# Flamingo block on one core: queries and keys split by row and turned by transposing transfers

## The reference

```python
x = x + tanh(g_xattn) * xattn(layernorm(x), ctx, ctx, 16)
x = x + tanh(g_ffn) * ffn(layernorm(x), w_gate, w_up, w_down)

def xattn(q, k, v, nh):          # v isn't rotated
    q = q * cos + rotate_half(q) * sin
    k = k * cos + rotate_half(k) * sin
    scores = einsum('bqhd,bkhd->bhqk', q, k) / sqrt(32) + slope[h] * (k_pos - q_pos)
    return einsum('bhqk,bkhd->bqhd', softmax(scores), v)
```

## Time and profile before

| | us |
|---|---|
| median of 3 runs (lowest, highest) | 1881.59 (1879.17, 1883.24) |
| the profiled execution | 1877.91 |
| its span, first to last instruction | 1876.1 |

### The profile page before, as it was taken

One profiled execution on the slowest core, in us unless ns is written; L12 is line 12 of the kernel. 1 busy time (PEld: TensorE's weight loads), 2 busy tenths in 40 slices (PEclk: granted clock), 3 DMA queues, 4 the chain that ended last, 5 costly groups with the idle time before them and its releaser, 6 DMA issues. The chain is left out here.

```text
span 1876.1 us, 25013 instructions
## 1 busy us (share of the span) xinstructions
PE 1682.4 (90%) x8927; PEld 635.5 (34%) x8927; DVE 1492.9 (80%) x2119; ACT 1184.3 (63%) x1898; POOL 809.8 (43%) x442
## 2 busy tenths in 40 slices
PE   2899999999999999999986999999999930499999
PEld 0223333323333333333222444444444410244444
DVE  6899888888888888888845998968889999865551
ACT  3476777777777777776662332328896689854440
POOL 4488888978889888888540020110000000000000
PEclk9899999999999999999998999999999975799999
DMA  5576877656776667765553988848994558855552
GB/s 159 137 182 155 186 181 179 153 135 144 178 179 151 156 150 170 172 150 122 116 168 77 275 270 239 242 160 263 277 294 136 149 202 289 265 196 170 169 170 71
DMA packets 234045, 339.51 MB, mean 181 GB/s; under 512 B 74400, under 2 KB 153120, under 8 KB 225664
## 3 DMA queue, kind: packets, MB, share of 16 engines
q1 hardware_dynamic: 224992, 272.89, 48.5%
q0 software_dynamic: 8928, 65.02, 17.4%
HBM read 164.04 MB, written 92.41 MB: 137 GB/s over the span
## 5 line engine op out<-in xcount | busy, mean ns | idle before, releaser
L1111 ACT ACTIVATE P<-quad 128x512 f32<-128x512 f32 x1024 | 557.3, 599 | 229.4 <-PE quad L928 225.7
L1308 DVE TENSOR_REDUCE cm<-quad 128x1 f16<-128x1024 f32 x512 | 601.1, 1216 | 84.3 <-PE quad L916 83.0
L1837 POOL TENSOR_TENSOR Ps<-P,P 128x2048 f32<-128x2048 f32 x93 | 422.8, 4546 | 151.4 <-ACT P L1111 151.4
L928 PE MATMUL quad<-QA,KA 101*128 101x512 f16 x1024 | 352.1, 385 | 7.1 <-ACT P L1111 6.0
L916 PE MATMUL quad<-KA,QA 100*128 100x512 f16 x1024 | 327.5, 390 | 26.4 <-DVE wh L1421 6.6
L964 PE MATMUL quad<-P,cg 128*32 128x512 f32 x2048 | 272.7, 604 | 3.6 <-ACT numT L1148 0.6
L1009 PE MATMUL quad<-x_hl,Wg 128*128 128x512 f16 x1152 | 249.3, 379 | 3.0 <-DMA x_hl<-xs 3.0
L1009 PE MATMUL quad<-x_hl,Wu 128*128 128x512 f16 x1152 | 248.8, 379 | 0.0
L1054 PE MATMUL quad<-Wd,oh 128*128 128x512 f16 x768 | 228.6, 379 | 0.0
L928 PEld LDWEIGHTS quad<-QA,KA 101*128 101x128 f16 x1024 | 85.9, 97 | 298.6 <-ACT P L1111 209.6
L1195 ACT ACTIVATE ev<-quad 128x1024 f32<-128x1024 f32 x96 | 97.3, 1014 | 125.2 <-PE quad L1009 119.2
(11 more groups left out here) (158 smaller groups left out, 1926.6 us busy)
## 6 DMA issues: line engine op xcount, KB each, us to landing
Ps<-P POOLq DMA_DIRECT2D x62, 1024.0 KB, 7.8
gate_scratch<-ev SPq DMA_DIRECT2D x48, 512.0 KB, 3.8
gt<-gate_scratch SPq DMA_DIRECT2D x48, 512.0 KB, 5.5
up_scratch<-ev SPq DMA_DIRECT2D x48, 512.0 KB, 3.1
uf<-up_scratch SPq DMA_DIRECT2D x48, 512.0 KB, 5.0
uf<-up_scratch SPq DMA_DIRECT2D x96, 256.0 KB, 3.6
QA<-part_scratch SPq DMA_DIRECT2D x45, 256.0 KB
KA<-part_scratch SPq DMA_DIRECT2D x45, 256.0 KB
```

The lines of the kernel that those rows point to most:

```text
L928: e.matmul(K.score[h % 2], K.KA[p % 2][0:101, h, 128 * kt:128 * kt + 128], K.QA[p % 2][0:101, qc, h, :], start=True, stop=True).then_inc(K ...
L1111: e.activation(K.Pb[pb][:, h, :], K.score[h % 2], ACT.Exp, scale=SCALE / (QPOW * KPOW)).then_inc(K.a_exp, 1)
L1308: e.tensor_reduce(cm[:, u:u + 1], K.quad[UNIT["max", hm, u] % 2][:, :], AX.X, ALU.max).then_inc(K.v_max, 1)
L1837: e.tensor_tensor(K.Ps[n][:, :, :], K.Pb[(st.g - 1) % NP][:, :, :], K.Pb[st.g % NP][:, :, :], ALU.add).then_inc(K.g_sum, 1)
```

## The change

Queries and keys are no longer turned by TensorE. The high part (ScalarE) and the low part (VectorE) are taken row by row from the rotated values in SBUF, and written straight into a stacked tile S of four slots per head: for queries high, high, low, constant; for keys high, low, high, constant with the bias in its first four columns. A transposing transfer from S, half of the rows at a time, then writes the operand. The operands are laid out by row tile: QA and KA are [128, 8, 4, 128]. The scale 2^-6 is put into the cosine and sine tables; the factor 2 for the queries into the deviation. The bias rows are turned once by TensorE at the start.

- The rotations change places: at w = 0, 2, 6 the keys, at w = 8, 10, 14 the queries of pair p+2.
- The normalization is for pair p+2, at w = 4, 5, 6, 7 (3, 1, 3 and 1 tiles).
- The parts: keys of p+2 at w = 10 and 12, queries of p+1 at w = 0 and 2, half of the rows at each.
- The transposing transfers for pair p+1: the keys' halves at w = 0 and 1, the queries' at w = 2 and 4. Each moves 128x2048 float16.
- The load of the context columns stays at w = 1, and stands on SP's queue between the keys' two transfers.
- At the start, the row deviations of the first batch are computed in two groups of four rows, and the first queries are rotated and split in two halves.

```diff
-NORM_TILES = {10: (0, 1), 12: (2, 3, 4), 14: (5, 6), 15: (7,)}
+NORM_TILES = {4: (0, 1, 2), 5: (3,), 6: (4, 5, 6), 7: (7,)}
...
-        if w == 8 and 0 <= p and p + 2 < NQ:
-            self.turn = (p + 2, 0)
-        elif w == 0 and 0 <= p and p + 1 < NQ:
-            self.turn = (p + 1, 1)
-        elif g == -7:
-            self.turn = (1, 0)
+        self.parts = None
+        if w in (10, 12) and -1 <= p and p + 2 < NQ:
+            self.parts = (p + 2, 1, (w - 10) // 2)
+        elif w in (0, 2) and 0 <= p and p + 1 < NQ:
+            self.parts = (p + 1, 0, w // 2)
...
-            self.rope = (p + 2, k // 3, k % 3)
+            self.rope = (p + 2, 1 - k // 3, k % 3)
...
-        self.stack = (p + 1, w - 1) if 0 <= p and 1 <= w <= 2 and p + 1 < NQ else None
+        self.stack = {0: (1, 0), 1: (1, 1), 2: (0, 0), 4: (0, 1)}.get(w) if 0 <= p and p + 1 < NQ else None
...
-    def load_stack(p, w):
+    def load_stack(p, w, half):
         if p >= 2:
             e.wait_ge(K.pe_score, score_no(2 * (p - 2) + 1, 7, 3))
...
+        if w:
+            e.wait_ge(K.a_kb, p + 1)
...
+        e.wait_ge(K.a_hi, part_no(p, w, half))
+        e.wait_ge(K.v_lo, part_no(p, w, half))
+        rows = slice(4 * half, 4 * half + 4)
+        dst = (K.QA, K.KA)[w][p % 2][:, rows, :, :].rearrange("c i h t -> c (i h) t")
+        e.dma_start_transpose(dst, K.S[w][:, rows, :, :, :].rearrange("t i h n d -> t (i h n d)")).then_inc(K.d_st[w][half], 16)
...
+    def high_part(p, w, half):
+
+        if p == 0 and w == 0:
+            e.wait_ge(K.v_rope0, 4 * half + 4)
+        else:
+            e.wait_ge(K.g_rope, rope_no(p, w))
+        if p > 0:
+            e.wait_ge(K.d_st[w][half], stack_no(p - 1))
...
+            e.activation(K.S[1][:, :, :, 3, 0:4], K.biasT[:, :, :, 4 * g:4 * g + 4].rearrange("t i n h -> t i h n"), ACT.Copy).then_inc(K.a_kb, 1)
+        src = K.t1[w][:, rows, :].rearrange("t i (h d) -> t (i h) d", d=HD).unsqueeze(2).to_broadcast([128, 16, 2, HD])
+        dst = K.S[w][:, rows, :, :, :].rearrange("t i h n d -> t (i h) n d")
+        dst = dst[:, :, 0:3:2, :] if w else dst[:, :, 0:2, :]
+        e.activation(dst, src, ACT.Copy).then_inc(K.a_hi, 1)
...
     def low_part(p, w, half):
-        c = slice(512 * half, 512 * half + 512)
-        e.wait_ge(K.a_hi, turn_no(p, w, half))
...
+        e.wait_ge(K.a_hi, part_no(p, w, half))
...
+        e.scalar_tensor_tensor(dst[:, :, 2 - w, :], src, 1.0, dst[:, :, 0, :], ALU.mult, ALU.subtract).then_inc(K.v_lo, 1)
```

More of the change, by code:

```diff
@@ L619, in load_stack @@
-    def load_stack(p, w):
+    def load_stack(p, w, half):
         if p >= 2:
             e.wait_ge(K.pe_score, score_no(2 * (p - 2) + 1, 7, 3))
-        e.wait_ge(K.d_part[w], 32 * p)
-        if p == 1 and w == 0:
+        if w:
+            e.wait_ge(K.a_kb, p + 1)
+        if p == 0 and half == 0:
             e.wait_ge(K.v_aux, 2)
[L625 to L633, removed]
@@ L714, in sync_program @@
     load_x_columns(1)
[L715 to L720, removed]
+    for w, half in ((1, 0), (1, 1), (0, 0), (0, 1)):
+        load_stack(0, w, half)
     load_context(2)
@@ L746, in sync_program @@
                     e.wait_ge(K.d_wh[h][i], 16 * 6)
-            e.wait_ge(K.d_st[1], 112 * 8)
+            for i in range(2):
+                for j in range(2):
+                    e.wait_ge(K.d_st[i][j], stack_no(NQ - 1))
             for i in range(2):
@@ L938, in tensor_program @@
     e.wait_ge(K.d_id, 16)
-    for w in (1, 0):
-        turn(0, w)
-    e.wait_ge(K.a_aux, 2)
+    e.wait_ge(K.d_bias, 16)
+    for i in range(8):
+        mm = e.transpose(K.score[0][:, 32 * i:32 * i + 32], K.bias[:, 128 * i:128 * i + 128], ident[0:32, 0:32])
+    mm.then_inc(K.pe_bias, 1)
     before = None
@@ L975, in tensor_program @@
                 mm.then_inc(done, 1)
-        if st.turn is not None:
-            turn(*st.turn)
         for job in st.side:
@@ L1157, in scalar_program @@
             exponent(st.hf, st.s, 3)
-        if st.turn is not None:
-            turned(*st.turn, 0)
-            turned(*st.turn, 1)
+        if st.parts is not None:
+            high_part(*st.parts)
         for job in st.side:
@@ L1317, in low_part @@
     def low_part(p, w, half):
[L1318 to L1328 removed]
+        rows = slice(4 * half, 4 * half + 4)
+        e.wait_ge(K.a_hi, part_no(p, w, half))
+        if p > 0:
+            e.wait_ge(K.d_st[w][half], stack_no(p - 1))
+        dst = K.S[w][:, rows, :, :, :].rearrange("t i h n d -> t (i h) n d")
+        src = K.t1[w][:, rows, :].rearrange("t i (h d) -> t (i h) d", d=HD)
+        e.scalar_tensor_tensor(dst[:, :, 2 - w, :], src, 1.0, dst[:, :, 0, :], ALU.mult, ALU.subtract).then_inc(K.v_lo, 1)
     def centre_x(n):
@@ L1337, in vector_program @@
         e.memset(K.cm[i][:, :], 0.0).then_inc(K.v_cm, 1)
+    e.memset(K.S[0][:, :, :, 3, :], QPOW * KPOW).then_inc(K.v_aux, 1)
+    e.memset(K.S[1][:, :, :, 3, :], -1.0).then_inc(K.v_aux, 1)
+    e.wait_ge(K.d_cs, 32)
+    for table in (K.cos, K.sin):
+        e.tensor_scalar(table[:, :, :], table[:, :, :], KPOW, None, ALU.mult).then_inc(K.v_cs, 1)
+    e.wait_ge(K.pe_bias, 1)
+    e.wait_ge(K.a_bias, 1)
+    bias = K.score[0][:, 0:256].rearrange("t (i n h) -> t i n h", n=2, h=16)
+    e.tensor_tensor(K.biasT[:, :, 2:4, :], bias, K.biasT[:, :, 0:2, :], ALU.subtract).then_inc(K.v_bias, 1)
@@ L1744, in gpsimd_program @@
     e.memset(K.seventh[:, :], 1.0 / 7.0).then_inc(K.g_half, 1)
+    e.memset(K.twice[:, :], QPOW / KPOW).then_inc(K.g_half, 1)
     e.memset(K.ones[:, :], 1.0).then_inc(K.g_ones, 1)
-    for part in range(3):
-        rope(0, 1, part)
     def step_of(out, a, b, op, sem, count):
```

265 lines of the change are left out of this document (102 added, 163 removed).

## The result

| | before | after |
|---|---|---|
| median, us (lowest to highest, runs) | 1881.24 (1879.17 to 1883.24, 4) | 1981.6 (1975.65 to 1996.85, 4) |
| profiled execution | 1877.91 | 1980.46 |
| its span | 1876.1 | 1977.6 |

The ratio is 1.0546, 95% interval 1.0485 to 1.0606. Forecast were 1881 and a range of 1860 to 1900; the change costs 100 us. Where the runs of one kernel spread, a ratio is taken from those within 1.5% of its fastest.

A forecast was written before the change was run, and what follows sets the result against it. TensorE was taken to bound attention. Terms: -34 (turns) -1.6 (key stack) +3 (ScalarE) +8 (VectorE) +25 (context) +2 (later accumulations) -3 (start) = -0.6 us, giving 1881 us on the median; range for 8 in 10, 1860 to 1900.

The forecast's parts named there:

- A low part reads SBUF instead of PSUM: VectorE's low parts: the source was given no price, since the same kind from SBUF takes 684 ns.
- the context wait: GpSimd's keys' rotation waits some 4 us for context columns, delaying the accumulating DMA and step 6's denominators on TensorE: +25.
- Steps 0 and 8: TensorE's steps with and without a turn: each turn costs 1.24 us; removing 29 gives -34, step 0 at 2.88.
- rival (c): TensorE isn't the bound, so the turns give nothing back: +33, 1915 us; chance 0.04.
- ScalarE's high part: Writes every value twice, 1.05 us four times a pair; about 0.2 us stick out at step 0: +3.
- Step 14: VectorE's low part at step 12 pushes the following maxima, so step 14 waits 0.6 us in 14 pairs: +8.
- The wait for the key stack of pair 1: The first maxima's wait of 1.61 us goes, since pair 1's keys are turned before step 0: -1.6.
- The start: Before the steps: constant rows and TensorE's turns go, row deviations and three transfers come: -3, bounds -8 and +5.
- upper bound for this stretch, 33.4: From step 0 to the accumulating DMA's landing, both landings at their most: 33.4 us, 10 a pair, 130 in all.
- Cost nothing: Four transposing transfers of 3.0 us a pair replace DRAM stores and seven loads, at no cost.
- Rival (b): Transposing transfers hold the engines, delaying context and accumulating DMA; 1.3 us more in 13 pairs gives 1898; chance 0.26.
- + 2: Later accumulations have 1 to 2 us less room, step 14's sharing engines with the first keys' transfer: +2 (0 to 13).

The follow-up runs named there:

- e1: Changed kernel, but the low part is a one-operand maximum from SBUF, the subtraction left out: 1930.6 us, ratio 1.0264.
- e2: Changed kernel with a fourth buffer for context columns, loaded a pair earlier; low parts as in the change: 1935.58 us, ratio 1.0286.
- e3: Changed kernel with one-operand low parts (subtraction left out) and context columns a pair earlier: 1901.38 us, 1877.52 to 1949.14 in ten runs, ratio 1.0048.
- e4: Kernel before the change, but the low part reads its first operand from the cosine table in SBUF instead of PSUM: 1959.06 us, ratio 1.0409.
- e9: e3, but GpSimd's transfer of exponent tiles 2 and 5 writes instead of accumulating: 1853.96 us, ratio 0.9852.
- e10: e3, but the four transposing transfers a pair are plain copies of the same size from a tile of zeros: 1856.14 us, ratio 0.9863.
- e6: e5 with the subtraction restored: ScalarE also writes the negated high part, VectorE adds both in a one-operand reduction: 1910.48 us, ratio 1.0156.
- e7: e6 with the keys' parts at steps 9 and 10 in place of 10 and 12: 1902.6 us, ratio 1.0143.
- e8: e5 with the subtraction restored and the low parts taken by GpSimd: 1903.0 us, ratio 1.0131.
- e5: e3 with the first keys' and last queries' transposing transfers kept apart from accumulating DMAs by waits and a later place: 1888.89 us, ratio 1.0045.

## Why the prediction was wrong

**The step that failed** is "A low part reads SBUF instead of PSUM. The same kind from SBUF takes 684 ns, so no price for the source." The row behind it is of the feed-forward, where GpSimd has next to nothing to do. In the attention GpSimd is busy 600 of 700 us, and there the same instruction took 680 to 4594 ns. Its price in the changed kernel is 51 us with the context wait present (after against e1). With it gone it is 34 by the medians of e2 and e3, or 43 by the six runs of e3 that its ratio is taken from; e3 is unsteady. The prediction did take the right duration for the instruction alone, but from a stretch in which the neighbour was idle; it asked what the instruction costs, not what it shares. The Trainium skill (SBUF — State Buffer, Who interferes with whom) has the rule: "A DVE instruction with two SBUF inputs contends with a GpSimd instruction that reads SBUF". By it every low part beside a rotation or a sum had to be priced with GpSimd's instruction. Before's low part had one operand in PSUM, so its durations could not show it. The trace agrees, e1 and e4 most directly.

**Points that held.** Steps 0 and 8 at 2.88 without their turns, so TensorE was the bound there and rival (c) is out. ScalarE's high part: 1.05 forecast, 1053 ns measured (two halves together took 1.2 before, not 1.05 as the prediction has it); step 1 after it 4.12 instead of 4.0, where 0.2 was forecast. Step 14 pushed by the low part's own length: 0.6 forecast, 0.59 in e1. The wait for the key stack of pair 1 is gone. The start: -3 forecast, -5.8 came.

**The context wait** was the right mechanism and undersized. The load was issued 3.01 us after step 0, and GpSimd went on 8.64 after step 0; the sum had 8.7 with the keys' transfer. But rotation to the DMA's issue took 9.79 instead of 9.3, with the sum of step 1 at 4.98 instead of 4.53, and issue to TensorE's start 9.04 instead of 7.8. The sum had put 25.8; it is 27.5 in pair 3. Where nothing else holds TensorE back, each of these us counts in full: forecast were +25 in all, and in e1 TensorE's waits for that DMA are 43.3. Undoing the wait gave 46 (after against e2, with the shorter holds of step 2 in it) and, by the medians, 29 or, by the six runs, 38 (e1 against e3). The prediction's upper bound for this stretch, 33.4, leaves out the 0.5 that its sum has; nothing rests on it.

**Transfers.** "Cost nothing" was the other failed step, smaller and hidden until e3: 47 us by the medians of e3 and e9, 38 by the six runs of e3. Rival (b), transposing transfers that hold back the accumulating DMA, named the mechanism, but as an even 1.3 us a pair and a price of 17. It came as rare landings of 16 to 28 us, which a sum over medians can't show. Its place in the changed kernel itself wasn't isolated; there the longest landings were 14.1 (accumulation) and 20.3 us (transposing). The 3.0 us put for one transposing transfer were short as well: the quickest landing in e9 is 4.2 us after issue.

**The sum, redone.** Without the context wait (+25) the prediction's own terms are -34 - 1.6 + 3 + 8 + 2 - 3 = -25.6, or 1856. e9 and e10, which have neither the held low parts, nor the context wait, nor the late landings, measured 1854 and 1856. So the terms that were worked out were right to 2 us together, and in part by luck. By the traces of before and e9, the steps from the first scores to the last give back 23.2 (-34 - 1.6 + 3 + 8 + 2 = -22.6 was forecast) and the start 5.7 (3 was), while the feed-forward takes 4.6 more, which nobody forecast: the last two misses cancel. What was wrong is three interactions, of which one was undersized and two stood at nothing. From after downwards the medians go 1981.6, 1935.6 (context early), 1901.4 (one operand; 1892.3 by the six runs), 1854.0 (no accumulation beside transposing). The parts depend on the order, so these are prices in this order, not shares.

Of e2, e6, e7 and e8 none beats the kernel before. Open: whether a third buffer for queries' and keys' operands, which would let all four transfers go between the accumulations, turns the 1.7 us a pair into a gain; that wasn't tried. Nor is it shown why only some of the transfers issued close together land late.

## What to carry to other kernels

When an edit moves an operand from PSUM to SBUF, price the instruction beside what runs on the neighbouring engine, not by its duration in a quiet stretch: look for rows of the same kind while GpSimd is busy, and if there are none, let the range reach to GpSimd's longest instruction, and beyond it where GpSimd runs without a gap. Before several transfers are put beside others, ask which kinds meet; a median landing time from a trace in which they never met says nothing about it. An interaction left at zero can be worth more than all the terms of a careful sum.

## What the runs showed of the hardware

- A two-operand SBUF instruction of VectorE that started while one of GpSimd ran ended some 0.55 us after a GpSimd instruction's end (after: 702.12 against 701.57, and 0.54 to 0.65 in all 52 held low parts; e4: 298.80 against 298.25). In most cases it is the end of the instruction that was running, but in e2 one was held for 11.72 us over five. GpSimd loses less: its sums take 4.53 us in the median and 5.11 at most, and the addition that began as the low part got through took 1.72 (701.52), where before none of its kind takes over 1.30.
- For 512 elements a partition, the one-operand reduction of e1 takes 674 to 689 ns beside a busy GpSimd, and the two-operand form in the feed-forward 679 to 693. The reduction over 1024 in e6 takes 1242.
- A transposing transfer of 128x2048 float16 from SBUF to SBUF lands 4.2 us after issue at the least and 4.9 in the median (e9). With accumulating DMAs of 1 MB in the same kernel, both kinds now and then land 16 to 29 us after issue (e3, e5), in e3 at 107 GB/s with the engines' share at 1.12; a load of weights beside them took 27.6 (e5). Without one of the two kinds the longest landings are 9.7 (e9) and 12.5 us (e10).
- Behind TensorE's waits of 2.49 us (after, pair 9) and 5.55 us (e1, pair 3) groups of eight take 1.93 and 1.94 us instead of 1.06, with the granted clock at 0.50; behind one of 4.00 (after, pair 3) the next group took 1.24. In pair 9 waits of 3.0 us together stand in a step that is 5.1 longer than the same step of e1.
